# A fused attention and mixture-of-experts kernel: the values product moved straight behind the next pair's scores

## The reference

```
xn  = layernorm(x)
lat = xn @ w_kv_down;  k, v = split(lat @ w_kv_up);  q = xn @ w_q      # 16 heads of 64
att = softmax(causal(q @ k.T / 8));  y = att @ v                       # per batch and head
out = x + y @ w_out
    + sum over 8 experts of where(token picked expert, mlp_e(xn) * wmean_e, 0)   # top 2 of 8
    + shared_mlp(xn)                                                   # silu(gate) * up, then down
```

## Time and profile before

| | us |
|---|---|
| median of 3 runs | 1014.62 |
| lowest, highest run | 1012.88, 1015.33 |
| span of the profiled execution | 995.0 |
| PE busy | 955.2 (96% of the span) |
| DVE busy | 707.6 (71%) |
| ACT busy | 651.3 (65%) |
| POOL busy | 339.3 (34%) |

### The profile page before, as it was taken

How to read it: one execution, slowest core, us unless ns; L and a number is a source line. 1 busy time by engine, 2 the same in 40 slices (tenths; PEclk the granted TensorE clock), 3 DMA queues, 4 the chain that set the end, 5 groups by cost and what they waited for, 6 DMA issues and landing times.

```text
span 995.0 us, 20239 instructions
## 1 busy us (share of the span) xinstructions
PE 955.2 (96%) x7200; PEld 768.4 (77%) x7200; DVE 707.6 (71%) x2016; ACT 651.3 (65%) x1801; POOL 339.3 (34%) x333
## 2 busy tenths in 40 slices
PE   5689998899999999999999999999999999999998
PEld 4456776787888888888888887888878778777776
DVE  5779699896666657666666756666576786888884
ACT  3747666665767666676667766677756775677771
POOL 0331113223233243443344433435131444444441
PEclk9799999999999999999999999999999999999999
DMA  6487424542225425465253552546433542533321
GB/s 194 163 308 244 162 102 146 164 169 82 100 81 181 144 96 171 119 201 181 86 181 118 183 187 92 151 154 181 160 101 126 165 129 73 180 108 105 124 86 43
DMA packets 66003, 142.77 MB, mean 143 GB/s; under 512 B 7856, under 2 KB 40880, under 8 KB 64112
## 3 DMA queue, kind: packets, MB, share of 16 engines
q1 hardware_dynamic: 52896, 91.77, 27.9%
q0 software_dynamic: 12432, 49.29, 15.9%
q10 hardware_dynamic: 576, 0.42, 0.1%
HBM read 104.76 MB, written 36.70 MB: 142 GB/s over the span
## 4 chain that ended last, share of the span: by engine, by line
PE 84%; issue 7%; DVE 6%; POOL 2%; DMA 1%; ACT 1%; DVEq 0%; POOLq 0%; SPq 0%
PE PS L670 15%; PE PS L671 14%; PE PS L672 14%; PE PS L712 13%; PE PS L703 13%; PE PS L693 12%; PE PS L819 2%; PE PS L811 1%; DVE pp L1245 1%; DVE acc L985 1%; DMA xs<-xs_scratch 1%; PE PS L718 1%; POOL rstd L1350 1%; DVE ohA L1196 1%; DVE acc L1158 0%
## 5 line engine op out<-in xcount | busy, mean ns | idle before, releaser
L924 ACT ACTIVATE pp<-pp,nmax 128x128 f32<-128x128 f32 (+3 forms) x512 | 280.7, 550 | 100.7 <-DVE nmax L1245 100.7
L1245 DVE CUSTOM_DVE_ANT_0 pp<-PS,maskw 128x128 f32<-128x128 f32 (+3 forms) x512 | 215.1, 483 | 4.7 <-PE PS L693 3.4
L1401 POOL TENSOR_TENSOR yy<-yf,yy 128x512 fp32r<-128x512 f32 x63 | 82.0, 1302 | 287.4 <-ACT yy L860 286.9
L703 PE MATMUL PS<-ident,pp 128*128 128x128 f32 x1280 | 165.1, 275 | 1.6 <-DVE acc L1215 1.5
L693 PE MATMUL PS<-qk 64*128 64x256 f32 (+2 forms) x1536 | 145.6, 335 | 15.9 <-issue 8.4
L703 PEld LDWEIGHTS PS<-ident,pp 128*128 128x128 f32 x1280 | 141.2, 141 | 16.7 <-issue 9.6
L712 PE MATMUL PS<-pt,vv 128*64 128x512 f32 (+3 forms) x1024 | 152.0, 439 | 0.0
L693 PEld LDWEIGHTS PS<-qk 64*128 64x128 f32 x1536 | 113.5, 189 | 31.4 <-issue 17.6
L712 PEld LDWEIGHTS PS<-pt,vv 128*64 128x64 f32 x1024 | 67.8, 136 | 90.4 <-issue 74.1
L860 ACT ACTIVATE pt<-PS 128x384 f32<-128x384 f32 (+1 forms) x215 | 108.5, 512 | 3.3 <-PE PS L703 3.2
L1251 DVE COPY pt<-PS 128x384 f32<-128x384 f32 x169 | 99.1, 591 | 12.8 <-PE PS L703 12.8
(11 more groups left out here) (169 smaller groups left out, 2072.1 us busy)
## 6 DMA issues: line engine op xcount, KB each, us to landing
rb<-rr_scratch SPq DMA_DIRECT2D x128, 128.0 KB
wr<-wm_scratch SPq DMA_DIRECT2D x16, 768.0 KB, 5.8
y_scratch<-acc SPq DMA_DIRECT2D x39, 256.0 KB
acc<-in_x SPq DMA_DIRECT2D x15, 512.0 KB, 5.9
wm_scratch<-hh SPq DMA_DIRECT2D x10, 768.0 KB, 4.0
xs_scratch<-wr SPq DMA_DIRECT2D x7, 1024.0 KB, 5.4
xs<-xs_scratch SPq DMA_DIRECT2D x7, 1024.0 KB, 4.8
xn_scratch<-acc SPq DMA_DIRECT2D x8, 512.0 KB, 3.4
```

Of the source, the lines that this page charges most:

```text
L703: done = e.transpose(o, pp[:, i % 4, P_AT[t] + 128 * kt:P_AT[t] + 128 * kt + 128], ident[:, :])
L924: e.activation(scores, scores, ACT.Exp, scale=-1.0, bias=nmax[:, b, t:t + 1], accum_out=rs[:, i % 4, 2 * t + h:2 * t + h + 1]).then_inc(a_ ...
L1245: e.tensor_tensor_reduce(pp[:, b, P_AT[t]:P_AT[t] + n], g[:, at:at + n], maskw[:, 512 - n:512], -1.0, 3e38, ALU.add, ALU.min, accum_out=nm ...
L1401: e.tensor_tensor(yy[:, i % 2, 1, :], yf[:, :], f32(yy[:, i % 2, 0, :]), ALU.subtract).then_inc(g_yl, 1)
```

## The change

In `work_order` the call `place(4 * P, end)` is moved from ahead of the `attend` piece to behind it. No piece is added, dropped or changed.

```diff
                 put("scores", P + 1, j)
                 tick()
-        place(4 * P, end)
         if 1 <= P <= NHT // 2:
             put("attend", P - 1)
             tick(1 if P < NHT // 2 else 8)
+        place(4 * P, end)
         for h in range(2):
```

## The result

| | before | after |
|---|---|---|
| median of 4 runs, us | 1014.98 (1012.88 to 1016.17) | 1023.65 (1021.37 to 1025.59) |
| profiled execution: span, its own time | 995.0 | 1023.8, 1025.59 |

The ratio is 1.0091, with a 95% interval from 1.0067 to 1.0116. The kernel became slower by 9 us, where 3.7 us less had been forecast.

The account below looks back on a forecast made before the run. PE was taken as the bound from about 200 us on; -8.0 (shape changes) + 3.3 (late waits) + 1.0 (odd waits) = -3.7 us, from 1014.62 to 1010.9 us. Own range 1008 to 1013; 8 in 10: 1005.5 to 1015.5.

Parts of the forecast that it names:

- The trace and the median: Whole run: 19.6 us lie around the profiled span of 995.0 and stay, so the span should come to 991.3.
- Shape changes on PE: PE, each step: one shape change fewer saves 0.15 us, counted in 53 steps from 200 us on, 8.0 us.
- the drain: PE leaving full width: 0.09 us saved a step, 4.8 us over 53 steps if only this is priced.
- The early steps: Nine steps before 200 us: a gain worth 1.3 us, counted at nothing since PE waits for others there.
- Rival 3: First 200 us: DVE idles 1.25 us ahead of the query's remainder in ten steps, costing 12.5 us, 1023; chance 0.12.
- Late filling work: Six late short steps: the later query makes the output projection wait 0.55 us for POOL's `yy`, 3.3 us in all.
- SP: Loads of expert weights behind a moved `down` start up to 2.3 us later, but stand several us ahead of use.
- Earlier values product: Values product, about 1.6 us earlier, needs DVE's copies `pt`; these come in time, so the cost is nothing.
- banks: Banks of moved pieces are freed later; no steady wait found, 1.0 us allowed for odd ones, bounds 0 and 3.
- Rival 1: Late steps: no late waits come, and the early steps' gain counts too, with 0.5 against it; 1005.8 us, chance 0.17.

Follow-up runs that it names:

- late: The new order only in the steps from 47 on (from about 780 us), the old order elsewhere, against the kernel before; ratio 0.9995.
- plain_from12: The kernel before with the new order from step 12 on and all POOL gathers replaced by plain transfers; 999.83 us, ratio 0.9845.
- plain_inner: The kernel before with plain transfers for gathers and the new order only in steps 12 to 47 without every eighth; 993.76 us, ratio 0.9971.
- plain_before: The kernel before, old order, with all 181 POOL gathers replaced by plain transfers of the same size; 995.77 us, ratio 0.9804.
- second trace of before: The kernel before, unchanged, profiled once more; span 1013.3 us, its own time 1015.11 us, ratio 0.9997.
- plain_rows_before: The kernel before, old order, with only the 64 late-stage gathers replaced by plain transfers; 997.07 us, ratio 0.9818.

## Why the prediction was wrong

**The trace and the median.** The forecast took the distance of 19.6 us between the span and the median for time around the span. 1.8 us lie there. The other 18 us were inside the usual run, in a mechanism that the first trace does not show. The sign that something was off stood in the table; a distance like that is a question, not a constant. It bore on the argument, since in the late stage of the usual run PE is not always the bound, and the forecast's terms for it are not seen (`late`: 0.9995, 0.9979 to 1.0012).

**Shape changes on PE.** The mechanism was right: distances, one change fewer, shown in the timeline. The size was right for the single step, 0.15 in 22 steps of 28, but six steps of the 28 gained nothing, so that the mean is 0.12 in `plain_from12` and 0.09 to 0.12 in `plain_inner`. The 53 steps counted begin with step 9, whose scores start at 187 us, inside the stage of the loss. The Trainium skill, TensorEngine Tiling (Array Packing), section Key Properties, says that a change of tiling mode drains the engine, and gives no price; the 0.09 a step that the forecast put on the drain came from its own rows. The 0.15 of the 22 steps says that the open weights count as well.

**The early steps.** This is the step that failed. They were counted at nothing, "since PE waits for others there anyway". That excludes a gain, not a loss: where PE waits for DVE, every delay of DVE lands on the end. They cost 10 us. Rival 3 named the place, the sign and nearly the time (1023); that the time fits is luck. It priced DVE's idle time at 1.25 us in each of ten steps, 12.5 in all. The trace has up to 1.51 at seven places, of which 3.2 us lie where the loss was made. The rest is what the rival had not: DVE's longer instructions beside POOL's (5.5 us; the distance falls from 10 to 12 to 3.6 without POOL's work) and the clock (3 to 4 us came back where it was held). These parts overlap, since a late remainder makes the wait and the wait lowers the clock, and do not add up. What was said against the rival, that the multiplication now comes without a wait, did not offset that.

**Late filling work.** Six late waits for POOL's `yy` were forecast at 0.55, in all 3.3. With signals on time `plain_from12` has them in place and number, at 0.51 by the distances: right. Not in the forecast is the key's remainder behind them, 0.25 each, 1.5 in all. In the usual run these waits drown in others: after shows four waits of 1.2 us for DVE's `pt` there, and the kernel before already waited five times for `yy` there, 1.5 us.

**SP.** The text let transfers stand "several us ahead of their use" and looked only at expert weights. SP loads the next batch's normed x once the last query of a batch is done, and that query came 2.3 us later in its step: 2.5 us in two waits of `plain_from12` (0.7 and 1.8), where `plain_before` has none. The queue was named, the wrong member of it was read.

**Earlier values product, banks.** For `pt` the values product waited 1.3 us once in after behind 230 us, close to nothing. The allowance of 1.0 for banks came true as two waits of 0.8 us (for `nmax`, which frees the bank of the values product at the pairs 25 and 33), and only where signals are held back. Rival 1's sum put these odd waits at 0.5 in place of 1.0; nothing hangs on that.

## What to carry to other kernels

Hold the profiled execution's own time against the runs before using it, and ask for a second trace where they differ by more than the 2 us around a span. Where the bounding engine waits for another, price every delay of that other engine at full, ask what runs beside its instructions, and count the clock that the wait can cost. Look up what is issued on the queues beside a stage that hangs on signals: here one wait that moved a burst of gathers behind the scores won 8.6 us on a chip with the hold, more than any order of the matmuls that was tried; on a chip without it the same wait cost 0.8.

## What the runs showed of the hardware

- Gathers issued by POOL held back the completion signals of PE on two of three chips. In the second trace of before 250 of the 462 completions that fell within 2 us behind a gather's start were over 0.15 us late, 4 of 991 others; on the second chip 159 of 327 (`plain_rows_before`). On the third chip and in the first trace 2 to 4 of 1453 were late. The price was 19.6 us in 1015. Plain transfers of the same bytes from the same queue held nothing (0 of 1453). Why chips differ was not tried.
- DVE's instructions from SBUF to SBUF took 1.1 us longer beside a POOL subtraction (0.42 to 1.58 and 1.53).
- PE's granted clock fell to half with or behind waits of 2.1 to 3.9 us (after, at 157, 171, 195 and 215 us), but not behind every such wait (2.35 us at 155 in the second trace of before). Scores took 3.89 us at it where they take 2.21. Filling such waits with matmuls without use kept the clock at 1.00 from 155 to 185 us.
- A wait of PE that the profile shows as 0.26 us moved the next start by 0.51, since the ends of matmuls are modelled.
- One wait of 0.7 us named `issue` stood ahead of a `gate_up` some 310 to 320 us in, in each kernel with the new order there and in none with the old one. It stays unexplained.
